# A transformer layer pair on one core: x also comes transposed, squares are added on VectorE, and the start waits for each constant by itself

## The reference

```python
qkv = x @ Wqkv                                   # block 1
q, k = apply_rope(q), apply_rope(k)
q = q / sqrt(sum(q * q, -1) + 1e-6);  k = k / sqrt(sum(k * k, -1) + 1e-6)
x = layernorm(x + softmax(q @ k.T / 4) @ v @ Wo + bo)
y = x                                            # block 2
y = y + softmax(q2 @ k2.T / 4) @ v2 @ w_proj     # q2, k2, v2 = layernorm(y) @ w_qkv
h = layernorm(y, ln2_w, ln2_b)
y = y + w2[e] @ gelu(w1[e] @ h)                  # e = argmax(h @ gate_w + gate_b)
out = layernorm(x + y)
```

## Time and profile before

| | us |
|---|---|
| median of 3 runs (lowest, highest) | 1502.35 (1497.89, 1505.28) |
| the profiled execution, its time | 1498.54 |
| its span, first to last instruction | 1496.6 |
| TensorE busy | 1320.7 (88%) |
| VectorE busy | 806.5 (54%) |
| ScalarE busy | 918.2 (61%) |
| GpSimd busy | 311.3 (21%) |

### The profile page before, as it was taken

How to read it: one execution, slowest core, us unless ns; L and a number is a source line. 1 busy time by engine, 2 the same in 40 slices (tenths; PEclk the granted TensorE clock), 3 DMA queues, 4 the chain that set the end, 5 groups by cost and what they waited for, 6 DMA issues and landing times. The chain is left out here.

```text
span 1496.6 us, 20966 instructions
## 1 busy us (share of the span) xinstructions
PE 1320.7 (88%) x7238; PEld 700.8 (47%) x7238; DVE 806.5 (54%) x1815; ACT 918.2 (61%) x1617; POOL 311.3 (21%) x247
## 2 busy tenths in 40 slices
PE   3499999999998898898989898999885599999993
PEld 1233443443443333333434343434322498999893
DVE  3333554454451767776777777777741343344341
ACT  0177787787786565555656666565551177777673
POOL 5122233333321111121212212122112111111111
PEclk9699999999999999999999999999986699999997
DMA  7221431432333131222121313121238211111113
GB/s 185 84 65 63 133 100 59 133 110 65 108 127 99 43 100 43 90 46 72 58 79 50 93 43 99 44 86 43 99 114 290 90 53 48 57 56 50 54 58 127
DMA packets 103495, 127.87 MB, mean 85 GB/s; under 512 B 7168, under 2 KB 91008, under 8 KB 103264
## 3 DMA queue, kind: packets, MB, share of 16 engines
q1 hardware_dynamic: 71568, 79.45, 16.8%
q10 hardware_dynamic: 27392, 33.56, 7.7%
q0 software_dynamic: 4432, 13.52, 2.5%
HBM read 51.51 MB, written 28.46 MB: 53 GB/s over the span
## 5 line engine op out<-in xcount | busy, mean ns | idle before, releaser
L642 ACT ACTIVATE w_space<-bank 128x512 f32<-128x512 f32 x1024 | 563.3, 599 | 378.1 <-PE bank L427 376.7
L841 DVE TENSOR_REDUCE negm<-bank 128x1 f32<-128x512 f32 x512 | 329.8, 684 | 123.4 <-PE bank L459 122.6
L427 PE MATMUL bank<-w_space 96*128 96x512 bf16 (+1 forms) x1024 | 361.1, 392 | 21.6 <-DMA w_space<-work_space 13.2
L444 PE MATMUL bank<-w_space 128*32 128x512 f32 x2048 | 277.9, 615 | 2.6 <-ACT w_space L651 2.3
L427 PEld LDWEIGHTS bank<-w_space 96*128 96x128 bf16 (+1 forms) x1024 | 94.9, 100 | 274.6 <-ACT w_space L642 176.1
L459 PE MATMUL bank<-w_space 96*128 96x512 bf16 x512 | 202.1, 395 | 22.1 <-DVE negm L841 13.3
L615 PE MATMUL bank<-w_space,work_space 128*128 x624 | 141.5, 380 | 0.0
L488 PE MATMUL bank<-work_space,wqkv_sb 128*128 128x512 f32 x256 | 126.9, 619 | 5.7 <-DVE w_space L968 4.8
L615 PEld LDWEIGHTS bank<-w_space,work_space 128*128 128x128 f32 x624 | 115.5, 190 | 14.4
L1188 POOL TENSOR_TENSOR work_space<-w_space,work_space 128x1024 bf16<-128x1024 f32 x32 | 68.1, 2128 | 189.6 <-ACT work_space L690 107.4
L459 PEld LDWEIGHTS bank<-w_space 96*128 96x128 bf16 x512 | 50.5, 99 | 116.8 <-DVE negm L841 79.0
(11 more groups left out here) (131 smaller groups left out, 1483.0 us busy)
## 6 DMA issues: line engine op xcount, KB each, us to landing
w_space<-work_space SPq DMA_DIRECT2D x384, 128.0 KB
w_space<-in_w_dram ACTq DMA_DIRECT2D x16, 1024.0 KB, 8.3
work_space<-rows_dram SPq DMA_DIRECT2D x39, 256.5 KB, 2.6
work_space<-in_x_dram ACTq DMA_DIRECT2D x16, 512.0 KB, 3.9
x_dram<-xo SPq DMA_DIRECT2D x16, 256.0 KB, 4.3
h_dram<-row_sb SPq DMA_DIRECT2D x16, 256.0 KB, 2.2
work_space<-h_dram ACTq DMA_DIRECT2D x8, 512.0 KB, 4.0
work_space<-x_dram ACTq DMA_DIRECT2D x8, 512.0 KB, 5.7
```

Source lines behind the costliest of these rows:

```text
L427: nc.tensor.matmul(bank[:, :], k_stack[0:rows, b % 2, HEADS_AT_ONCE * g + j, kt * P:(kt + 1) * P], q_stack[0:rows, b % 2, HEADS_AT_ONCE * ...
L444: last = nc.tensor.matmul(pv_bank[VW * j:VW * (j + 1), :], v_aug[:, b % 2, at:at + VW], probs[:, q % PROBS, j, :], start=(kt == 0), stop=( ...
L642: nc.scalar.activation(probs[:, q % PROBS, j, :], st_bank(b, c)[0][:, :], ACT.Exp, scale=SCALE).then_inc(exps, 1)
L841: ve.tensor_reduce(negm[:, c % TT, c // TT:c // TT + 1], mx_ring.bank(b, (g, c))[:, :], axis=AX.X, op=ALU.max, negate=True).then_inc(mx_ri ...
```

## The change

- A second input, x_t, is x with tokens last, prepared by the host. For block 1, T0 and T1 are gone; the projections read x_t, in two buffers used in turn (xT and the place of x_sb), loaded on ScalarE's queue. The load of batch b waits for V1 of batch b-2.
- New tasks aq and ak on VectorE add the two halves of the squares in place; nq and nk are one matmul each, and wait for `sq_added`.
- The table of block 1 is laid out anew.
- Batch 0 takes a PSUM bank of its own for each of its eight projection tasks, and a second place for the rotated k (`trig_of`), so that k waits for no read-out of q.
- The Q and K columns of the weights are loaded first, with a semaphore of their own; cos and sin go on ScalarE's queue. TensorE begins on w_in and x_in, VectorE on trig_in; the other constants are waited for where they are used (ahead of nq of batch 0, or of stage 1).
- The rows of ones in k_stack come by DMA (ones_pairs), not by GpSimd's memset. VectorE's casts of identity and pad stand at the start of stage 1; the 9 padding stores are issued at the start of SP's stage 2, and waited for ahead of VectorE's N2 in block 1.
- The stack copies are issued part by part, each as soon as its part is ready, in order high, middle, low; for k of batch 0 ScalarE's queue issues them.
- `group_out` stands at j = 1 in place of j = 3.

```diff
 PROJECTED = (
-    dict(T0=(0, 0), T1=(0, 2), qA=(1, 3), qB=(2, 2), kA=(3, 3), kB=(4, 2), sq=(4, 2), nq=(5, 3),
-         sk=(6, 0), uq=(6, 2), hq=(6, 3), nk=(7, 0), lq=(7, 1), uk=(8, 1), hk=(8, 2), lk=(9, 0),
+    dict(qA=(0, 3), qB=(1, 2), kA=(2, 3), kB=(3, 3), sq=(3, 3), aq=(4, 3), nq=(6, 0), sk=(6, 1),
+         uq=(7, 1), ak=(7, 2), hq=(7, 2), lq=(8, 0), nk=(8, 2), uk=(9, 2), hk=(9, 3), lk=(10, 1),
          V0=(12, 0), V1=(14, 0)),
...
-        N_FIRST, N_LATER, N_CONST_OPS = 7, 12, 4
+        N_FIRST, N_LATER, N_CONST_OPS = 5, 13, 3
...
-        p_ring = Ring("proj", [psum[4]], sem)
+        p_ring = Ring("proj", [psum[i] for i in (4, 0, 1, 2, 3, 5, 6, 7)], sem)
...
-                            p_ring.add(b, name, 0)
+                            p_ring.add(b, name, 0 if b else len(p_ring.uses))
...
+        def x_transposed(b):
+
+            return xT if second(b) or b % 2 else xT_of_x
+
+        def trig_of(b, qk):
+
+            return probs[:, 0, :, :] if b == 0 and qk else trig
...
+        def stack_copies(eng, b, qk):
+
+            stack, slots = ((q_stack, Q_SLOTS), (k_stack, K_SLOTS))[qk]
+            wait(eng, scores, CHUNKS * (b - 1))
+            for part in range(3):
+                if part == 0 and second(b):
+                    eng.wait_ge(high_done, 4 * (b - BATCH) + (2 * qk + 2))
+                elif part == 0:
+                    eng.wait_ge(p_step, 2 * SPLIT_STEPS * b + (SPLIT_STEPS * qk + 4))
+                elif part == 1:
+                    eng.wait_ge(mid_done, 2 * b + (qk + 1))
+                else:
+                    eng.wait_ge(parts_ready, 2 * b + (qk + 1))
+                for slot in range(len(slots)):
+                    for half in range(2 if slots[slot] == part else 0):
+                        eng.dma_start(stack[2 * slot + half:STACK:ROW_STEP, b % 2, :, :],
+                                      parts[:, qk, part, half, :]).then_inc(stack_in[qk], 16)
...
         def _(pe):
-            pe.wait_ge(consts_in, 16 * N_FIRST)
-            pe.wait_ge(consts_set, N_CONST_OPS)
+            pe.wait_ge(w_in, 16 * KD)
...
-                    pe.wait_ge(sq_done, 2 * b + (1 if name == "nq" else 2))
-                    for k in range(2):
-                        last = nc.tensor.matmul(bank[:, :], head_sum_sb[:, :], sq[:, k, :],
-                                                start=(k == 0), stop=(k == 1))
+                    if b == 0 and name == "nq":
+                        pe.wait_ge(consts_in, 16 * N_FIRST)
+                    pe.wait_ge(sq_added, 2 * b + (1 if name == "nq" else 2))
+                    last = nc.tensor.matmul(bank[:, :], head_sum_sb[:, :], sq[:, 0, :],
+                                            start=True, stop=True)
...
                 if n == 1:
                     pe.wait_ge(later_in, 16 * N_LATER)
-                    pe.wait_ge(pool_set, 2)
+                    pe.wait_ge(consts_set, N_CONST_OPS)
+                    pe.wait_ge(ident_ready, 1)
+                    pe.wait_ge(pool_set, 1)
...
+                elif name == "lk" and b == 0:
+                    stack_copies(act, b, 1)
...
-                if b:
+                if b > BATCH:
                     act.wait_ge(*p_ring.full(b - 1, "T1"))
+                elif b > 1:
+                    act.wait_ge(*p_ring.full(b - 2, "V1"))
...
             load_x(0)
+            act.dma_start(cos_sb[:, :], cos_t).then_inc(trig_in, 16)
+            act.dma_start(sin_sb[:, :], sin_t).then_inc(trig_in, 16)
...
-                        if j == 3:
+                        if j == 1:
                             for b, g in group_copied(n, q):
                                 group_out(b, g)
...
-            dve.wait_ge(consts_in, 16 * N_FIRST)
-            ve.tensor_copy(ident_bf[:, :], ident_sb[:, :]).then_inc(consts_set, 1)
-            ve.tensor_copy(row_sb[:, 0, 2 * D:ROW].bitcast(U32), pad_c
-                           ).then_inc(pad_set, 1)
...
+            dve.wait_ge(trig_in, 32)
...
-                if name in ("T0", "T1") and not second(b):
-                    dve.wait_ge(*p.full(b, name))
-                    ve.tensor_copy(xT[:, u, :], p.bank(b, name)[:, :]
-                                   ).then_inc(p.drain_sem(b, name), 1)
+                if name in ("aq", "ak"):
+                    dve.wait_ge(sq_done, 2 * b + ("qk".index(name[1]) + 1))
+                    ve.tensor_tensor(sq[:, 0, :], sq[:, 0, :], sq[:, 1, :], ALU.add
+                                     ).then_inc(sq_added, 1)
...
-            pool.memset(k_stack[STACK:STACK + NEG, :, :, :], 1.0).then_inc(pool_set, 1)
...
-            pool.wait_ge(consts_in, 16 * N_FIRST)
...
+            for k in range(KD):
+                sp.dma_start(wqkv_sb[:, 0, k, 0:2 * D], w_qkv1[k * P:(k + 1) * P, 0:2 * D]
+                             ).then_inc(w_in, 16)
...
+                if n == 2:
+                    sp.wait_ge(pad_set, 2)
+                    for e in range(E + 1):
+                        sp.dma_start(rows_dram[e * ROOM:e * ROOM + P, :], row_sb[:, 0, :]
+                                     ).then_inc(padded, 16)
```

More of the change, by code:

```diff
@@ L141, in wait, with program @@
         eng.wait_ge(sem, value)
-def program(nc, x, w_qkv1, w_o1, b_o, ln1_w, ln1_b, w_qkv2, w_o2, ln2_w, ln2_b, gate_w, gate_b,
-            w1, w2, cos_t, sin_t, head_sum, ident, route_consts, out):
+def program(nc, x, x_t, w_qkv1, w_o1, b_o, ln1_w, ln1_b, w_qkv2, w_o2, ln2_w, ln2_b, gate_w, gate_b,
+            w1, w2, cos_t, sin_t, head_sum, ident, route_consts, ones_pairs, out):
     ctx = ExitStack()
@@ L480, in task @@
                 elif name in ("qA", "qB", "kA", "kB"):
-                    if name == "qA":
+                    if name == "qA" and second(b):
                         pe.wait_ge(*ring.empty(b, "T0"))
                         pe.wait_ge(*ring.empty(b, "T1"))
+                    elif name == "qA":
+                        pe.wait_ge(x_in[b % 2], 16 * (b // 2) + 16)
                     c = ("qA", "qB", "kA", "kB").index(name)
@@ L745, in load_x @@
                         act.wait_ge(stored, 16 * (b - BATCH + 1))
-                act.dma_start(x_sb[:, :, :], tiles(h1_dram if second(b) else x, b % BATCH)
-                              ).then_inc(x_in, 16)
+                    act.dma_start(x_sb[:, :, :], tiles(h1_dram, b % BATCH)).then_inc(x_in[b % 2], 16)
+                else:
+                    act.dma_start(x_transposed(b)[:, :, :], x_t[b].rearrange("(k p) t -> p k t", p=P)
+                                  ).then_inc(x_in[b % 2], 16)
             def load_residual(b):
@@ L964, in task @@
                         dve.wait_ge(*p.full(b, name))
-                        wait(dve, rot_done, 2 * b + qk)
+                        if b:
+                            dve.wait_ge(rot_done, 2 * b + qk)
+                        turned = trig_of(b, qk)
                         first, then = (sin_sb, cos_sb) if half else (cos_sb, sin_sb)
-                        ve.tensor_tensor(trig[:, 2 * half, :], bank[:, :], first[:, :], ALU.mult)
-                        ve.tensor_tensor(trig[:, 2 * half + 1, :], bank[:, :], then[:, :],
+                        ve.tensor_tensor(turned[:, 2 * half, :], bank[:, :], first[:, :], ALU.mult)
+                        ve.tensor_tensor(turned[:, 2 * half + 1, :], bank[:, :], then[:, :],
                                          ALU.mult).then_inc(p.drain_sem(b, name), 1)
@@ L1179, in task @@
                     wait(pool, parts_ready, 2 * b + (qk - 1))
[L1180 removed]
+                    turned = trig_of(b, qk)
+                    pool.tensor_tensor(rest[:, qk, 0, :], turned[:, 0, :], turned[:, 2, :],
                                        ALU.subtract)
[L1182 removed]
+                    pool.tensor_tensor(rest[:, qk, 1, :], turned[:, 1, :], turned[:, 3, :], ALU.add
                                        ).then_inc(rot_done, 1)
@@ L1266, in _ @@
                 (gate_w_sb[:, 0, :], gate_w[0:P, :]), (gate_w_sb[:, 1, :], gate_w[P:D, :]),
-                (gate_b_sb[:, :], gate_b.partition_broadcast(P)))
+                (gate_b_sb[:, :], gate_b.partition_broadcast(P)),
+                (w1_space[STACK:STACK + NEG, H * T:2 * H * T], ones_pairs))
             assert (len(first), len(later)) == (N_FIRST, N_LATER)
@@ L1272, in _ @@
                 sp.dma_start(dst, src).then_inc(later_in, 16)
-            sp.wait_ge(pad_set, 2)
-            for e in range(E + 1):
-                sp.dma_start(rows_dram[e * ROOM:e * ROOM + P, :], row_sb[:, 0, :]
-                             ).then_inc(padded, 16)
             def task(name, b):
@@ L1283, in task @@
                     qk = "qk".index(name[1])
-                    stack, slots = ((q_stack, Q_SLOTS), (k_stack, K_SLOTS))[qk]
-                    sp.wait_ge(parts_ready, 2 * b + (qk + 1))
-                    wait(sp, scores, CHUNKS * (b - 1))
-                    for slot, part in enumerate(slots):
-                        for half in range(2):
```

(8 more changed lines are left out.)

40 lines of the change are left out of this document (24 added, 16 removed).

## The result

The changed kernel takes 1452.4 us (median of 4 runs, 1450.04 to 1458.37) against 1502.11 us before; the ratio is 0.968, 95% interval 0.964 to 0.972. Its profiled execution took 1454.59 us for a span of 1452.8 us. The forecast was 1448 us.

What follows compares the result with a forecast made beforehand. TensorE's own stream was taken to bound the first half, a chain through all engines the start; 1498.5 - 29 (start) - 25 (batches 1 to 7) = 1444.5, plus 3.8 is 1448 us, range 1437 to 1468.

Steps and rivals of the forecast that it cites:

- TensorE's first instruction: Start: TensorE waits only for x_t and the Q/K columns, taken as 6 us, against 17.24 us before.
- The chain of the start: Start: projections through stack copies to batch 0's first score at 41.5 us instead of 70.2, a gain of 29 us.
- worst case: Start: the DMA engines serve both copy lists as one, 24 x 0.67 from 25.5 us, first score at 45.0.
- The sign for the first score: Start: the first score at 37 to 46 us would show the forecast.
- T0, T1 and the halved head sums: Batches of block 1: transposes gone, 0.87 us, and one matmul fewer per head sum, 1.72 us a batch.
- The stall: Batches of block 1: second head sum's wait for the squares, 0.99 us a batch, counted as gone.
- Rival (a): First half: ScalarE becomes the bound, steady gain shrinks to nothing, 1473 us; chance 0.09.
- The oT copy: Copy moved from place 3 to 1: may hold ScalarE's exps, zero to 64 us lost, taken as nothing.
- Rival (b): The early oT copy makes ScalarE hold exps and costs TensorE: 64 us lost against 54 won, 1512 us; chance 0.04.
- The stack copies by part: Every batch: SP issues high copies before the others are ready, earlier and never later; costed at nothing.
- (c): Second half: SP's waits in the copy lists delay neg_T stores, 2 us a batch, 1464 us; chance 0.07.
- (d): Start: colliding loads keep the change from shortening it; at 8 us and cold, 1457 us; chance 0.08.

Runs made afterwards that it cites:

- the extra-copies run: Changed kernel with 12 more copies of the same form behind batch 0's 12 Q copies on SP's queue: 1458.32 us, ratio 0.967.
- the repetition: The changed kernel unchanged, run again on another experiment chip: 1453.3 us, ratio 0.972 to the kernel before.
- The reintroduced head sums: Changed kernel with nq and nk in two matmuls each again and without VectorE's two adds: 1462.57 us, ratio 0.974.

## Why the prediction was right, and where it was off

The range (1437 to 1468) and the direction held; the forecast was 4.4 us low. Like with like it was further off: it was made against the profiled execution, as 1444.5 us, and the changed kernel's profiled execution took 1454.59 us, 10.1 more. The difference of the medians hides 6 us of that, since the median before lay 3.8 us above its profiled execution and the median after 2.2 us below. By its steps:

- **TensorE's first instruction** at 6.38 us against 6 forecast: right. The cast was what it had waited for; memset and cast went together, so how much of the cast's 8.19 us the memset made isn't shown.
- **The chain of the start** was right to the first copy, though two errors nearly cancel in it (the last two of this item). The term that was mis-sized is the one for which no row stood: K's copies on ScalarE's queue. I took Q's and K's lists as independent, with the shared list as worst case (45.0 us); the extra-copies run shows that they share one rate of some 0.67 us a copy, and 45.0 was the case. It came out at 43.9 or 46.9 us, 1.3 us of that by the clock. The sign for the first score, 37 to 46 us, was missed in the first profile and met in the repetition. The projections were faster than assumed (9.58 us to the end against 11.5), aq slower (1.60 us against 0.65, beside GpSimd's tensor operation, itself 1.71 instead of 1.26).
- **T0, T1 and the halved head sums**, 2.6 us a batch: right on TensorE's stream, where they measure 2.67 us. The reintroduced head sums show that only 7.4 of their 12.0 us reach the time.
- **The stall**: this step failed. The wait on the squares went, as forecast, but 1.31 us of listed waits and 0.15 us in the scores' gaps came in its place. I had compared ScalarE's work with the batch as a whole (84%); it is full for 14 us in every 51, where the new table leaves TensorE less work than ScalarE has, and four banks don't carry TensorE over that. Rival (a) was thus right in mechanism for a quarter of each batch, and the forecast for the rest; by the prediction's own sign, a period above 51 us with waits on exps, it is (a), but its price, no steady gain at all, is not what came. That sign and the 49.3 us rest on 52.9 us for the batch before, which took 53.50. With 1.5 us a batch lost in seven, the 25 us became 14.4, and the 3.6 us of batch 8 make 18.0.
- **The oT copy**, costed at nothing with up to 64 us of loss: the sign was wrong. It saves 12 us in the new kernel, for a reason the rows hinted at (L444 had waited 1.1 us for it once) and I read as proof that it didn't matter. A resource that is waited for now and then before can be waited for often when the waiting engine gets faster. Rival (b) is out.
- **The stack copies by part**, costed at nothing: they carry 15 us of the change. About 7 of these are a wait of the kernel before that I had not read, 3.6 us ahead of batch 8's first max score, and the half clock after it; the rest keeps the new kernel's batches from running into their copies. Block 2, forecast unchanged, gained 4.1 us, 3.6 of them behind that wait. From the first score of batch 8 on, the mark that the prediction named, the length did stay (982.3 us before, 983.5 after).
- **Rivals (c) and (d)** did not come about: waits on neg_T are 8.0 us in all, against 7.8 before, and the first matmul came at 6.4 us.

That the total came so near is in part luck, beyond the 6 us of the medians: an unread gain of 7.7 us stood against 6 us less at the start and 11 us less in the steady batches, and the gain from the copy's place is contained in a steady term that I had ascribed to the matmuls alone.

## What to carry to other kernels

When one engine is the bound and you shorten its stream, compare the next engine's load with the new stream stretch by stretch, not over the whole period: where it is full, the gain stops. Steps that free a buffer for the bounding engine (here the PSUM copy and the stack copies) can be worth nothing while it is slow, as the PSUM copy was, and carry the gain once it is faster, so cost them at the new pace. And take a period between two of the same wait in steady batches, not as a mean that takes in the first. Splitting one list of transfers over two queues doesn't make it shorter unless a row shows that the two move more bytes together.

## What the runs showed of the hardware

- Copies of 1 KB rows into 8 partitions moved 184 GB/s from one queue and 172 to 192 from SP's and ScalarE's together, at a DMA share of 0.53 to 0.55, and 178 to 183 GB/s at 0.68 to 0.70 with GpSimd's queue beside ScalarE's. An issue on a queue took 0.61 to 0.62 us in the median with nothing beside it and up to 1.4 us when another queue competed.
- A fp32 add of 128x512 on VectorE took 1.44 to 1.60 us, once 2.71, when it started beside a GpSimd tensor operation, and 0.69 us without, in the same kernel; the GpSimd operation behind it took 1.71 to 1.74 instead of 1.26 us.
- The clock in the start differs between executions of one kernel: the first head sum ran at 2.04 or at 1.10 us for the same two records. With the projections before it, that moved the first stack copy by 1.3 us.
